# Transformer layer with mixture of experts: the shared expert in plain fp32, the second norm and the router's tail rearranged

## The chip, the cores and the metric

One core of a Trainium2 chip runs the kernel. The metric is the device time of the whole program in microseconds; three runs of the kernel before gave 993.31, 994.20 and 994.36 us, median 994.2 us.

## The reference

One pre-norm transformer layer over 2048 tokens of width 128, in fp32. Biases and weight scales are as drawn.

```python
x = x + attn(layernorm(x), qkv_w, qkv_b, out_w, out_b)       # 16 heads of 64, causal softmax
x = x + ffn(layernorm(x), gate_w, expert_*, shared_*)

def _ffn(x, gw, uw, dw):                                     # width 352
    return jax.nn.silu(x @ gw.T) * (x @ uw.T) @ dw.T
shared = _ffn(xf, shared_gate, shared_up, shared_down)
probs = softmax(xf @ gate_w.T)                               # 8 experts
topw, topi = top_k(probs, 2); topw = topw / (topw.sum(-1) + 1e-20)
out = shared + sum over the two chosen experts of topw * _ffn(xf, expert weights)
```

## The kernel before

The residual is held feature-major (128 features on the partitions, 2048 tokens along the free axis, four blocks of 512). Products that need fp32 accuracy are made of three matmuls in fp32r, whose operands are split into a high and a low part (`mm3`: high x high, high x low, low x high).

**Attention.** The loop over 16 heads (`for h in range(H)`) runs over 20 groups of two key tiles each (`GROUPS`). TensorE writes scores into `st`, which has two halves (`STRING`), so it can be two groups ahead; ScalarE makes the exponential twice, in fp32 and fp16; GpSimd subtracts one from the other (`p_low`); three groups later (`LAG`) TensorE multiplies by V (`p_times_v`). Beside that, `SLOTS[h][n]` lists by hand the background tasks of each place. Each task uses one of three banks of `bg` in turn, made on TensorE and drained on VectorE in the order of `TASKS`; a bank is used anew when the third task before has been drained (`bg_drained`). In the last head (`LAST_HEAD`), where there is no next head to prepare, all tasks stand behind both scores of their group and ahead of its mask.

**Last head.** For a block of 512 tokens: `att_t` (transposes the last pair's attention rows; waits for `normalise`), `att_y` (output projection, added to `res`), `turn` (transposes `res` to token-major; VectorE takes the statistics and copies it back into `res`), `inverse_deviation` (the second norm's factor by two Newton steps, on VectorE, for 8 tiles at once), `normal_rows`, `rows_t` (transposes the normalised rows back, split into high and low part), `logits`, `router_top`, `ranks` (positions of the tokens in their expert's list, by matmuls with a triangle and ones), `places`. `second_copy` makes a copy of the rows for the second chosen expert. Each row has two more words: its number and its weight (`ROW` = 130).

**Shared expert.** 12 steps (`STEPS`, four blocks by three chunks of 128 hidden features): gate and up by `mm3`, SiLU on ScalarE, `hidden` on VectorE, `hidden_hi` on ScalarE, `hidden_lo` on VectorE, `down` by `mm3` two steps later, `shared_copy`, and `base`: transposed and added to `res`. The rest of the tasks of blocks 2 and 3 are placed between the steps. GpSimd then scatters the rows with indirect DMAs (`scatter_rows(g)`, 16 for each half of the tokens) to lists in DRAM by expert. `early_table` and `late_table` make the table of the 39 tiles: the expert and the first row of each; the first `EARLY` = 9 of them are from the first half alone.

**Expert tiles.** For each of 39 tiles of 128 rows: SP gathers it (`XRING` = 8 buffers; gather i waits until the result of tile i-8 has been stored), TensorE transposes it, gate and up, SiLU, product, transposes, down; the result is scaled by the row's weight and scattered to `y_dram` by GpSimd (`scatter_y`). At the end SP loads the results in four parts, VectorE adds two rows for each token, and SP stores.

Of the kernel before, what the change touches and what calls it, by code (L numbers as in the profile page):

```python
# [12 lines left out]
F32, F32R = mybir.dt.float32, mybir.dt.float32r  # L13
# [23 lines left out]
HRING, SRING = 2, 2  # L37
# [4 lines left out]
XRING, YRING, AHEAD = 8, 12, 2  # L42
SKIP = 8192
ROW = P + 2
# [4 lines left out]
FILLS = 8  # L49

# [46 lines left out]
def background(h):  # L97
# [17 lines left out]
    if h + 1 < H:  # L115
# [19 lines left out]
TAIL = [("ranks", 0), ("att_t", PAIRS - 1, 3), ("att_y", PAIRS - 1, 3), ("turn", 2), ("turn", 3), ("rows_t", 2),  # L135
        ("rows_t", 3), ("base", 0), ("logits", 1), ("base", 1), ("ranks", 1), ("base", 2), ("base", 3)]
# [15 lines left out]
def layer_kernel(nc, x_t, qkv_w, qk_bias_in, v_bias, out_w, out_bias, gate_w_t, ffn_w, out_rows):  # L152
    ctx = ExitStack()
    with ctx:
# [57 lines left out]
        lg = sb("lg", [P, NT, EXPERTS], F32)  # L212
        lg_max = sb("lg_max", [P, NT, 1], F32)
        pr = sb("pr", [P, NT, EXPERTS], F32)
# [3 lines left out]
        top_atf = sb("top_atf", [P, NT, 2], F32)  # L218
        top_w = sb("top_w", [P, NT, 2], F32)
        wsum = sb("wsum", [P, NT, 1], F32)  # L220
        hot = sb("hot", [P, 2, NT, EXPERTS], F32)

        shared_hi = sb("shared_hi", [P, 3 * FC * P], F32R)
        shared_lo = sb("shared_lo", [P, 3 * FC * P], F32R)
# [8 lines left out]
        newton = sb("newton", [P, 3, 8], F32)  # L233
        shifted = sb("shifted", [P, 8], U32)
# [3 lines left out]
        chosen_sum = sb("chosen_sum", [P, 3, EXPERTS], F32)  # L238
        ones = sb("ones", [P, P], F32)
        tri = sb("tri", [P, P], F32)  # L240
# [12 lines left out]
        shared_raw = pflat[:, 2 * 2 * BLK:2 * 2 * BLK + 3 * FC * P]  # L253


        second = [v_words[0][:, 4 * ROW * b:4 * ROW * (b + 1)] for b in range(NB - 1)] + [high_words[:, 0:4 * ROW]]
        second = [x.rearrange("p (t c) -> p t c", c=ROW) for x in second]
# [3 lines left out]
        chosen = wo_flat[:, 0:P].rearrange("p (t e) -> p t e", e=EXPERTS)  # L261
        slot_at = wo_flat[:, P:2 * P].rearrange("p (t e) -> p t e", e=EXPERTS)
        hot_slot = wo_flat[:, 2 * P:4 * P].rearrange("p (r t e) -> p r t e", r=2, e=EXPERTS)
        reach = wo_flat[:, 4 * P:5 * P].rearrange("p (e j) -> p e j", e=EXPERTS)
        ends_by = wo_flat[:, 5 * P:5 * P + DUMP * EXPERTS].rearrange("p (i e) -> p i e", e=EXPERTS)
# [4 lines left out]
        place = wr_flat[0][:, 96:128].rearrange("p (r t) -> p r t", r=2)  # L270
        tiles_past = wr_flat[0][:, 192:192 + DUMP]
        row_sum = wr_flat[0][:, 240:240 + DUMP]
        row_base = wr_flat[0][:, 288:297]
        row_step = wr_flat[0][:, 304:312]
        taken = wr_flat[0][:, 312:320]
        gap = wr_flat[0][:, 320:329]
        count_now = wr_flat[0][:, 344:352]
# [3 lines left out]
        h_hi = [split_flat[:, k * BLK:(k + 1) * BLK] for k in range(HRING)]  # L281
        h_lo = [stage_parts[:, k * BLK:(k + 1) * BLK] for k in range(HRING)]
# [4 lines left out]
        shared_t = low_words[:, YRING * P:YRING * P + BLK]  # L287
        t_y_low = [high_words[:, 4 * ROW + k * P:4 * ROW + (k + 1) * P] for k in range(2)]
# [8 lines left out]
        t_x_hi = [shared_hi[:, k * P:(k + 1) * P] for k in range(2)]  # L297
        t_x_lo = [shared_hi[:, (2 + k) * P:(3 + k) * P] for k in range(2)]
# [37 lines left out]
        router_max, router, router_exp = sem("router_max"), sem("router"), sem("router_exp")  # L336
        shared_landed, shared_hi_ready, shared_lo_ready = sem("shared_landed"), sem("shared_hi_ready"), sem("shared_lo_ready")
# [3 lines left out]
        ln_stats, ln_rows, rows_ready = sem("ln_stats"), sem("ln_rows"), sem("rows_ready")  # L341
        turned_copied, hot_ready, places_ready = sem("turned_copied"), sem("hot_ready"), sem("places_ready")
        table_ready, shared_copied = sem("table_ready"), sem("shared_copied")
# [7 lines left out]
        y_landed, y_added, out_ready = [sem(f"y_landed{b}") for b in range(NB)], sem("y_added"), sem("out_ready")  # L351
        gu_ready, silu_done, h_ready = sem("gu_ready"), sem("silu_done"), sem("h_ready")
        h_hi_ready, h_lo_ready, down_done = sem("h_hi_ready"), sem("h_lo_ready"), sem("down_done")
# [21 lines left out]
        def v_quad(slot, q, lo, hi):  # L375
            return v_parts[slot][:, :, 4 * q:4 * q + 4, lo:hi]
        def stage_width(j):
            return F if j < 2 else FC * P
# [10 lines left out]
        def tiles_of(g):  # L389
            return slice(8 * g, 8 * g + 8)  # L390

# [4 lines left out]
        def _(sp):  # L396
# [13 lines left out]
            sp.dma_start(shared_raw, ffn_w[SHARED, :, :]).then_inc(shared_landed, 16)  # L410

            def spread_head(h):

# [1092 lines left out]
```

## Time and profile before

| | us |
|---|---|
| median of three runs | 994.2 |
| the profiled execution | 994.17 |
| its span | 992.4 |
| TensorE busy (share) | 924.8 (93%) |
| VectorE busy | 740.9 (75%) |
| GpSimd busy | 729.9 (74%) |
| ScalarE busy | 713.3 (72%) |

Fifteen heads take up to 761.7 us, the last head up to 817.6, the shared expert with the router's tail up to 884.5, the tiles up to 977.6, and the end is 14.8 us. A busy share is a mean over these; a wait row names the instruction that waited, and the one that released it. A matmul's duration in the rows contains its drain, which overlaps the next one: the distance between two starts is the pace. A fp32 matmul shows as two records.

### The profile page before, as it was taken

The page shows a single profiled execution, that of the slowest core. Times are in us where ns is not written, and L with a number is a line of the kernel's source. Part 1 is how long each engine was busy: PE and PEld are TensorE (multiplying, and loading weights), DVE is VectorE, ACT ScalarE, POOL GpSimd, SP SyncE. Part 2 cuts the span into 40 slices and gives each one's busy share as a digit, 9 for nine tenths or more (in the row PEclk, how much of TensorE's full clock was granted, in tenths as well). Part 3 has the DMA queues.
Part 4 walks back from the last instruction along what each step waited for, and adds up shares of the span by engine and source line. Part 5 has one row for each costly group of instructions (what it writes and reads, how often), then busy time and mean ns, then how long its engine had stood idle before and what let it go on. Part 6 is the DMA issues. An engine that isn't in the chain of part 4 may idle for free. (4 is left out here: it accounts for less than half of the span.)

```text
span 992.4 us, 25979 instructions
## 1 busy us (share of the span) xinstructions
PE 924.8 (93%) x10330; PEld 776.1 (78%) x10330; DVE 740.9 (75%) x1775; ACT 713.3 (72%) x891; POOL 729.9 (74%) x460
## 2 busy tenths in 40 slices
PE   7889999999999999999999999999999787779992
PEld 5458888888888888888888888888887575669992
DVE  4978797878878786978797868778784667756664
ACT  4048888888888888788888888898889752335661
POOL 1328888888898888888989888898889845064442
PEclk8879999999999999999999999999999978879996
DMA  3321434343544444535414040404032015111214
GB/s 104 85 64 23 94 77 118 78 109 78 118 88 99 98 112 104 124 84 122 105 39 111 31 110 25 117 25 102 6 83 99 39 69 192 31 44 52 58 56 135
DMA packets 70103, 82.03 MB, mean 83 GB/s; under 512 B 8784, under 2 KB 53970, under 8 KB 67936
## 3 DMA queue, kind: packets, MB, share of 16 engines
q1 hardware_dynamic: 67712, 76.14, 31.1%
q0 software_dynamic: 2272, 4.24, 1.2%
q8 instruction: 84, 1.38, 0.6%
q14 instruction: 35, 0.29, 0.1%
HBM read 21.81 MB, written 25.30 MB: 47 GB/s over the span
## 5 line engine op out<-in xcount | busy, mean ns | idle before, releaser
L583 POOL TENSOR_TENSOR p_lo<-prob,p_hi 128x1024 f16<-128x1024 f32 x320 | 617.5, 1947 | 136.9 <-ACT p_hi L685 135.7
L684 ACT ACTIVATE prob<-st,p_bias 128x1024 f32<-128x1024 f32 x320 | 329.7, 1030 | 124.4 <-PE st L1276 98.0
L685 ACT ACTIVATE p_hi<-st,p_bias 128x1024 f16<-128x1024 f32 x320 | 327.7, 1024 | 0.0
L979 DVE TENSOR_REDUCE row_max<-bg 128x1 f32<-128x512 f32 x384 | 255.4, 685 | 14.6 <-PE bg L1201 9.1
L1275 PE MATMUL st<-big 128*128 128x512 f32 (+3 forms) x640 | 242.8, 382 | 3.0 <-ACT p_hi L685 1.7
L1201 PE MATMUL bg<-big 128*128 128x512 f32 (+3 forms) x640 | 236.5, 400 | 4.5 <-DVE v_parts L969 2.1
L1307 PE MATMUL pv<-v_parts,p_hi 128*128 128x65 f16 x2176 | 235.9, 194 | 1.8 <-POOL p_lo L583 1.8
L1307 PEld LDWEIGHTS pv<-v_parts,p_hi 128*128 128x128 f16 x2176 | 200.5, 96 | 45.5 <-issue 32.6
L1309 PE MATMUL pv<-v_parts,p_hi 128*128 128x64 f16 x2176 | 234.6, 195 | 0.0
L1276 PE MATMUL st<-big 65*128 65x512 f32 (+3 forms) x640 | 233.2, 370 | 0.0
L1311 PE MATMUL pv<-v_parts,p_lo 128*128 128x65 f16 x2176 | 233.0, 192 | 0.0
L1311 PEld LDWEIGHTS pv<-v_parts,p_lo 128*128 128x128 f16 x2176 | 203.4, 99 | 0.0
L1309 PEld LDWEIGHTS pv<-v_parts,p_hi 128*128 128x128 f16 x2176 | 203.1, 97 | 0.2
L1201 PEld LDWEIGHTS bg<-big 128*128 128x128 f32 x640 | 124.0, 194 | 33.7 <-DVE row_max L979 7.7
L1275 PEld LDWEIGHTS st<-big 128*128 128x128 f32 x640 | 122.9, 192 | 19.0 <-ACT p_hi L685 2.8
L1276 PEld LDWEIGHTS st<-big 65*128 65x128 f32 x640 | 122.3, 191 | 17.8
L975 DVE CUSTOM_DVE_ANT_0 junk<-bg,mask_wide 128x128 bf16<-128x128 f32 (+3 forms) x256 | 121.9, 483 | 9.6 <-PE bg L1201 8.4
L959 DVE TENSOR_SCALAR big<-bg,qk_bias 128x512 fp32r<-128x512 f32 x64 | 48.0, 750 | 68.3 <-PE bg L1154 68.3
L618 POOL DMA_INDIRECT y_dram<-p_lo,v_parts x39 | 37.8, 970 | 50.2 <-DVE p_lo L1123 50.2
L961 DVE SCALAR_TENSOR_TENSOR big<-bg,qk_bias,big 128x512 fp32r<-128x512 f32 x64 | 48.1, 751 | 2.3
L611 POOL DMA_INDIRECT row_dram<-attn,place_u x16 | 16.3, 1017 | 35.6 <-DVE place_u L893 23.4
L1132 DVE TENSOR_TENSOR prob<-prob,st 128x352 f32<-128x352 f32 x39 | 20.3, 521 | 28.5 <-ACT prob L759 28.5
(224 smaller groups left out, 1227.9 us busy)
## 6 DMA issues: line engine op xcount, KB each, us to landing
big<-big SPq DMA_DIRECT2D x192, 128.0 KB, 2.3
row_dram<-fill SPq DMA_DIRECT2D x8, 1300.0 KB, 9.4
big<-part_dram SPq DMA_DIRECT2D x8, 1088.0 KB, 7.8
big<-big SPq DMA_DIRECT2D x16, 512.0 KB, 4.3
part_dram<-stage_parts SPq DMA_DIRECT2D x32, 176.0 KB, 3.2
part_dram<-stage_parts SPq DMA_DIRECT2D x16, 192.0 KB, 3.8
stage_raw<-ffn_w SPq DMA_DIRECT2D x16, 176.0 KB, 3.0
v_parts<-row_dram SPq DMA_DIRECT2D x39, 65.0 KB, 1.8
```

What stands on the lines that cost most here:

```text
L583: nc.gpsimd.tensor_tensor(o, a, b, ALU.subtract).then_inc(p_lo_ready, 1)
L684: nc.scalar.activation(o32, src, ACT.Exp, bias=p_bias[:], scale=D ** -0.5)
L685: nc.scalar.activation(o16, src, ACT.Exp, bias=p_bias[:], scale=D ** -0.5).then_inc(exp_done, 1)
L961: nc.vector.scalar_tensor_tensor(out=q_lo_shift[s][:, blk(b)], in0=bank, scalar=bias, in1=k_lohi[s][:, blk(b)].bitcast(F32), op0=ALU.add, ...
L975: nc.vector.tensor_tensor_reduce(masked[k % BGRING][:, 0:width], bank[:, 0:width], mask_wide[:, BLK - width:BLK], 1.0, -3.0e38, ALU.add, A ...
L979: nc.vector.tensor_reduce(row_max[:, t, c:c + 1], bank, AX_X, ALU.max).then_inc(bg_drained, 1)
L1201: mm = nc.tensor.matmul(bank[:, 0:width], q_hihi[s][:, tile(t)], k_lohi[s][:, c * BLK:c * BLK + width], start=True, stop=True)
L1275: nc.tensor.matmul(out, k_lohi[s][:, tile(kt)], q_hihi[s][:, q], start=True, stop=False)
L1276: mm = nc.tensor.matmul(out, k_hi_one[s][0:D + 1, tile(kt)], q_lo_shift[s][0:D + 1, q], start=False, stop=not diagonal)
L1307: nc.tensor.matmul(out, p_hi[:, n % PRING, cols], v[:, 0:D + 1], start=(kt == 0 and j == 0), stop=False, skip_group_check=True)
L1309: nc.tensor.matmul(out[:, 0:D], p_hi[:, n % PRING, cols], v[:, D + 1:VW], start=False, stop=False, skip_group_check=True)
L1311: mm = nc.tensor.matmul(out, p_lo[:, n % PRING, cols], v[:, 0:D + 1], start=False, stop=(kt == 4 * b + j), skip_group_check=True)
```

## The change

- The shared expert's gate, up and down products are made in fp32, one matmul for three: `shared_hi`, `shared_lo`, `h_hi`, `h_lo` and the operations that made them go; `shared_w` comes. The hidden ring `HRING` is 3.
- The result of the down product is added to `res` while that is feature-major (`base_sum`, VectorE); `base` then transposes the sum, and ScalarE copies it to `res` (`base_copy`). `turn` no longer writes `res`.
- The last pair's output projection is one fp32 matmul (`att_whole`).
- The second norm: `turn` itself makes the inverse deviation of blocks 0 and 1, each for four tiles with intermediate results in a PSUM bank, and the normalised rows from PSUM. Blocks 2 and 3 are done together in `turn` 3. `rows_t` makes only `xn`, no high and low parts; for blocks 2 and 3 ScalarE copies.
- The router takes the two largest logits themselves from PSUM; `router_exps` and the weights are computed once, after the tiles, and applied to the results at the end. Rows have 129 words. `ranks` works in bf16; `places` has fewer steps.
- The tasks have other places: `LAST_HEAD` starts one place earlier, with `ranks` 0 and `turn` 2 in it; the steps of the shared expert are written out by hand. The late table is made in tile 2 of the expert tiles.
- `XRING` is 12. The end works in eight chunks (`CHUNKS`), with 32 scaled additions. The last expert's weights are loaded without a wait for `att_y`. `second_copy` is ScalarE's, and the scatters go first over the first choices, then over the second.

```diff
-HRING, SRING = 2, 2
+HRING, SRING = 3, 2
-XRING, YRING, AHEAD = 8, 12, 2
+XRING, YRING, AHEAD = 12, 12, 2
-LAST_HEAD = {6: [("att_t", PAIRS - 1, 0)], 7: [("att_y", PAIRS - 1, 0)], 8: [("turn", 0)],
-             9: [("att_t", PAIRS - 1, 1)], 10: [("att_y", PAIRS - 1, 1)], 11: [("turn", 1)],
-             13: [("rows_t", 0)], 15: [("rows_t", 1)], 16: [("att_t", PAIRS - 1, 2), ("logits", 0)],
-             17: [("att_y", PAIRS - 1, 2)]}
+LAST_HEAD = {5: [("att_t", PAIRS - 1, 0)], 6: [("att_y", PAIRS - 1, 0)], 7: [("turn", 0)],
+             9: [("att_t", PAIRS - 1, 1), ("rows_t", 0)], 10: [("att_y", PAIRS - 1, 1)], 11: [("turn", 1)],
+             13: [("rows_t", 1)], 15: [("att_t", PAIRS - 1, 2)], 16: [("logits", 0)], 17: [("att_y", PAIRS - 1, 2)],
+             18: [("ranks", 0)], 19: [("turn", 2)]}
...
+            def inverse_deviation(t0, n, scratch):
+                t = slice(t0, t0 + n)
+                aside = [newton[:, 2 + k, 0:n] if scratch is None else scratch[:, 8 * k:8 * k + n] for k in range(3)]
+                variance, halved, copy = aside
+                own(nc.vector.tensor_scalar(variance, mean_var[:, t, 1], EPS, None, ALU.add))
...
+                y, square = newton[:, 0, 0:n], halved
+                for k, constant in enumerate(RSQRT_STEPS):
+                    other = y
+                    if scratch is not None:
+                        other = copy
+                        own(nc.vector.tensor_copy(copy, y))
+                    own(nc.vector.tensor_tensor(square, other, y, ALU.mult))
+                    own(nc.vector.tensor_tensor(square, square, var_half[:, 0:n], ALU.mult))
...
+                    if b < 2:
+                        att = ("att_y", PAIRS - 1, b)
+                        inverse_deviation(4 * b, 4, bg[:, NUMBER[att] % BGRING]).then_inc(bg_drained, 1)
+                        dve.wait_ge(bg_drained, drained(att))
+                        rows_of(attn, bank, b).then_inc(bg_drained, 1)
...
-                mm3(pv[:, :], shared_hi[:, d], shared_lo[:, d], h_hi[q % HRING], h_lo[q % HRING],
-                    c == 0, c == FC - 1).then_inc(down_done, 1)
+                nc.tensor.matmul(pv[:, :], shared_w[:, (2 * FC + c) * P:(2 * FC + c + 1) * P], h32[q % HRING], start=(c == 0),
+                                 stop=(c == FC - 1)).then_inc(down_done, 1)
...
-                mm3(st[:, q % 2, 0, :], shared_hi[:, g], shared_lo[:, g], xn_hi[:, blk(b)], xn_lo[:, blk(b)], True, True)
-                mm3(st[:, q % 2, 1, :], shared_hi[:, u], shared_lo[:, u], xn_hi[:, blk(b)], xn_lo[:, blk(b)], True, True
-                    ).then_inc(gu_ready, 1)
+                nc.tensor.matmul(st[:, q % 2, 0, :], shared_w[:, g], xn[:, blk(b)], start=True, stop=True)
+                nc.tensor.matmul(st[:, q % 2, 1, :], shared_w[:, u], xn[:, blk(b)], start=True, stop=True
+                                 ).then_inc(gu_ready, 1)
...
+            def base_sum(b):
+                dve.wait_ge(down_done, FC * (b + 1))
+                nc.vector.tensor_tensor(res[:, blk(b)], res[:, blk(b)], pv[:, :], ALU.add).then_inc(shared_summed, 1)
...
+            router_weights()
+            rows = res[:, :].rearrange("p (t d) -> p t d", d=P)
+            for c in range(CHUNKS):
+                dve.wait_ge(y_landed[c], 16)
+                for r in range(2):
+                    for t in range(NT)[chunk(c)]:
+                        last = nc.vector.scalar_tensor_tensor(out=rows[:, t], in0=y_rows[:, t, r, :], scalar=top_w[:, t, r:r + 1],
+                                                              in1=rows[:, t], op0=ALU.mult, op1=ALU.add)
```

The new order on TensorE in the shared expert, written out: gate/up 0, att_t 3, gate/up 1, att_y 3, gate/up 2, turn 3, down 0, gate/up 3, down 1, gate/up 4, down 2, gate/up 5, rows_t 2, rows_t 3, down 3, down 4, logits 1, down 5, gate/up 6, gate/up 7, ranks 1, down 6, base 0, gate/up 8, down 7, base 1, gate/up 9, down 8, gate/up 10, down 9, base 2, gate/up 11, down 10, down 11, base 3.

## Rows read from the trace of the kernel before

**Rows 1.** Windows: stretch, length, busy of PE, PEld, DVE, ACT, POOL, clock, DMA.
```profile
761.70:817.60 55.90, 44.52 (x605) 37.36 (x602) 32.34 (x98) 39.51 (x42) 40.58 (x22) 0.88 0.22 83
817.60:884.50 66.90, 46.34 (x209) 36.31 (x205) 46.29 (x174) 20.75 (x36) 27.92 (x28) 0.86 0.28 100
884.50:977.60 93.10, 87.90 (x623) 84.53 (x622) 57.32 (x155) 53.89 (x155) 41.66 (x44) 0.96 0.18 51
977.60:992.40 14.80, 0.00 (x0) 0.00 (x0) 5.53 (x8) 0.00 (x0) 0.94 (x1) 0.50 0.69 213
```

**Rows 2.** Waits, 758 to 822: who waited for whom, total us, times, longest.
```profile
ACT prob L684 <- PE st L1276: 12.4, 6, 8.5
...
PE bg L1228 <- DVE attn L824: 6.8, 1, 6.8
...
ACT prob L684 <- PE st L1288: 2.6, 3, 2.2
```

**Rows 3.** Timeline, last head: start, us, engine, line, operation.
```profile
789.34 4.20 POOL L583 TENSOR_TENSOR p_lo<-prob,p_hi 128x1024 f16<-128x1024 f32 x2 [0.29 <-ACT p_hi L685]
789.52 1.97 DVE L813 TENSOR_TENSOR newton<-newton 128x8 f32<-128x8 f32 x1
...
791.52 2.04 DVE L814 TENSOR_TENSOR newton<-newton,var_half 128x8 f32<-128x8 f32 x1
...
794.41 2.14 DVE L824 TENSOR_SCALAR attn<-res,mean_var,rstd 128x128 f32<-128x128 f32 x8
```

**Rows 4.** Timeline, VectorE, shared expert: statistics and inverse deviation.
```profile
832.29 0.89 DVE L998 BATCH_NORM_STATS2 stats<-bg 128x6 f32<-128x128 f32 x4
...
836.46 0.17 DVE L813 TENSOR_TENSOR newton<-newton 128x8 f32<-128x8 f32 x1
```

**Rows 5.** The page's costliest groups: busy, mean ns; idle before, releaser.
```profile
L684 ACT ACTIVATE prob<-st,p_bias 128x1024 f32<-128x1024 f32 x320 | 329.7, 1030 | 124.4 <-PE st L1276 98.0
```

**Rows 6.** Timeline, TensorE: fp32 first norm and V, fp32r in the shared expert.
```profile
4.04 6.22 PE L1159 MATMUL st<-res,ones_mean 128*128 128x512 f32 x8 [4.04 <-DMA res<-x_t]
...
698.04 1.05 PE L1191 MATMUL bg<-w_raw,xn 128*128 128x128 f32 x8
...
824.02 0.40 PE L1153 MATMUL st<-xn_lo,shared_hi 128*128 128x512 f32 x1
...
824.26 0.40 PE L1154 MATMUL st<-xn_hi,shared_lo 128*128 128x512 f32 x1
```

**Rows 7.** Windows, two pieces at the lower clock, columns as in rows 1.
```profile
818.00:822.00 4.00, 4.00 (x19) 3.53 (x17) 1.50 (x8) 0.60 (x1) 0.00 (x0) 0.57 1.00 418
...
863.00:872.50 9.50, 9.21 (x32) 8.18 (x33) 4.65 (x16) 1.10 (x2) 1.95 (x3) 0.50 0.15 39
```

**Rows 8.** Timeline, GpSimd: second half's first scatter, stores of tiles 0, 11, 12, 38.
```profile
869.95 0.97 POOL L611 DMA_INDIRECT row_dram<-attn,place_u  x1 [23.43 <-DVE place_u L893]
...
893.41 0.97 POOL L618 DMA_INDIRECT y_dram<-p_lo,v_parts  x1 [2.92 <-DVE p_lo L1123]
...
918.69 0.97 POOL L618 DMA_INDIRECT y_dram<-p_lo,v_parts  x1 [1.13 <-DVE p_lo L1123]
920.79 0.97 POOL L618 DMA_INDIRECT y_dram<-p_lo,v_parts  x1 [1.13 <-DVE p_lo L1123]
...
977.57 0.97 POOL L618 DMA_INDIRECT y_dram<-p_lo,v_parts  x1 [1.32 <-DVE p_lo L1123]
```

**Rows 9.** Timeline of the end: loads of the results, first and last additions.
```profile
979.83 2.03 SPq L503 DMA_DIRECT2D big<-y_dram  x4
983.81 0.69 DVE L1143 TENSOR_TENSOR res<-res,big 128x512 f32<-128x512 f32 x1 [7.01 <-DMA big<-y_dram]
...
989.01 0.69 DVE L1145 TENSOR_TENSOR res<-res,big 128x512 f32<-128x512 f32 x1
```

**Rows 10.** Groups by line, 817 to 884.2: busy, mean ns, idle before and releaser.
```profile
L1070 DVE TENSOR_TENSOR stage_parts<-prob,split 128x512 fp32r<-128x512 f32 x12 | 8.2, 684 | 1.7 <-ACT split L716 1.7
```

More of the change, by code:

```diff
@@ L134 @@
 PROLOGUE += [("v", 0, q) for q in range(4)] + max_tasks(0) + [("shift", 0)]
-TAIL = [("ranks", 0), ("att_t", PAIRS - 1, 3), ("att_y", PAIRS - 1, 3), ("turn", 2), ("turn", 3), ("rows_t", 2),
-        ("rows_t", 3), ("base", 0), ("logits", 1), ("base", 1), ("ranks", 1), ("base", 2), ("base", 3)]
+TAIL = [("att_t", PAIRS - 1, 3), ("att_y", PAIRS - 1, 3), ("turn", 3), ("rows_t", 2), ("rows_t", 3), ("logits", 1),
+        ("ranks", 1), ("base", 0), ("base", 1), ("base", 2), ("base", 3)]
 STAGED = [(e, j) for e in range(EXPERTS) for j in range(3)]
@@ L482, in _ @@
             sp.wait_ge(st_ready, H * NG)
-            for e in range(3, 7):
+            for e in range(3, EXPERTS):
                 expert_weights(e)
-            sp.wait_ge(bg_ready, drained(("att_y", PAIRS - 1, 3)))
-            expert_weights(7)
             for i in range(TILES):
@@ L624, in _ @@
             pool.wait_ge(filled, 16 * FILLS)
-            for g in range(2):
-                scatter_rows(g)
+            scatter_rows(0)
+            scatter_rows(1)
             for i in range(TILES):
@@ new lines, in places @@
+                own(nc.vector.tensor_tensor(
+                    hot_slot, hot[:, g], bank[:, 0:8 * EXPERTS].rearrange("p (o t e) -> p o t e", o=1, e=EXPERTS).broadcast_to(
+                        [P, 2, 8, EXPERTS]), ALU.mult))
+                with nc.allow_low_precision(reason="one whole number and zeros"):
+                    nc.vector.tensor_reduce(place_u[:, :, t], hot_slot, AX_X, ALU.add).then_inc(places_ready, 1)
+                nc.vector.tensor_copy(count[g], bank[:, 8 * EXPERTS:9 * EXPERTS]).then_inc(bg_drained, 1)
@@ new lines, in _ @@
+            background_task(("turn", 3))
+            hidden(2)
+            hidden(3)
+            early_tiles()
+            hidden(4)
+            base_sum(0)
+            table(0, EARLY)
+            hidden(5)
+            background_task(("logits", 1))
+            hidden(6)
+            base_sum(1)
+            background_task(("ranks", 1))
+            hidden(7)
+            early_taken()
+            hidden(8)
+            hidden(9)
+            late_tiles()
+            hidden(10)
+            base_sum(2)
@@ L1110, in tile_x_lo @@
+            hidden(11)
+            base_sum(3)
             def tile_x_lo(i):
@@ L1253, in background_task @@
                     b = task[1]
[L1254 removed]
+                    pe.wait_ge(shared_summed, b + 1)
                     for t in range(4):
[L1256 removed]
+                        mm = nc.tensor.transpose(bank[:, tile(t)], res[:, tile(4 * b + t)], ident[:])
                     mm.then_inc(bg_ready, 1)
@@ new lines, in _ @@
+            background_task(("att_t", PAIRS - 1, 3))
+            gate_up_shared(1)
+            background_task(("att_y", PAIRS - 1, 3))
+            gate_up_shared(2)
+            background_task(("turn", 3))
+            down(0)
+            gate_up_shared(3)
+            down(1)
+            gate_up_shared(4)
+            down(2)
+            gate_up_shared(5)
+            background_task(("rows_t", 2))
+            background_task(("rows_t", 3))
+            down(3)
+            down(4)
+            background_task(("logits", 1))
@@ L1393, in _ @@
+            down(5)
+            gate_up_shared(6)
+            gate_up_shared(7)
+            background_task(("ranks", 1))
+            down(6)
+            background_task(("base", 0))
+            gate_up_shared(8)
+            down(7)
+            background_task(("base", 1))
+            gate_up_shared(9)
+            down(8)
+            gate_up_shared(10)
+            down(9)
             background_task(("base", 2))
-            for q in range(STEPS - FLAG, STEPS):
-                down(q)
+            gate_up_shared(11)
@@ L1396, in _ @@
+            down(10)
+            down(11)
             background_task(("base", 3))
```

518 lines of the change are left out of this document (222 added, 296 removed).

## The prediction

> **What bounds the kernel now.** I read four views in this order. First the busy time by stretch [rows 1]: up to 761.7 us TensorE is busy nearly all the time, and the change touches nothing there that anything waits for (one split of the output weights in head 13, the two splits of the shared weights at the start, long before their use). From 761.7 us on no engine is full. So the reader should look at four stretches: the last head (55.9 us), the shared expert with the router (66.9 us), the 39 expert tiles (93.1 us), the end (14.8 us). What counts in each is who waits for whom.
>
> In the last head, ScalarE waits for scores for 12.4 us and 2.6 us more [rows 2], 15.0 us together, and TensorE for the normalised rows (L824) for 6.8 us in one piece. The timeline of that piece [rows 3] shows why: inside the inverse deviation two operations on 128x8 take 1.97 and 2.04 us, while GpSimd runs its subtraction of 4.20 us for two. The same operation without GpSimd's subtraction takes 0.17 us [rows 4]. Both read both inputs from SBUF.
>
> In the second stretch TensorE is busy 46.3 of 66.9 us, VectorE 46.3 [rows 1]; work goes to and fro between three engines (gate, SiLU, product, high part, low part, down), and TensorE's granted clock falls to 0.5, its 1.2 GHz level, after each longer idle piece: 4 us at 818 and 9.5 us at 863 [rows 7]. In the third TensorE sets the pace (87.9 of 93.1 us busy).
>
> **The change part by part.** *Last head.* The inverse deviation of blocks 0 and 1 moves into the task that turns the block, keeps its intermediate results in a PSUM bank, and the normalised rows are read from PSUM too. So no operation of it has two SBUF inputs. 13 operations at 0.17 us and 0.03 between, 0.2 each [rows 4], are 2.6 us; with four bn_stats (0.89) [rows 4], their aggregation with its waits (taken as 0.6) and four rows at 0.27 (2.14 for eight, [rows 3]) the task is 5.5 us of VectorE. It comes twice now, at places 7 and 11, and the next block's normalise and transpose queue behind it on VectorE. TensorE can be two groups ahead (the two halves of the score banks), some 4 us of ScalarE, whose two exponentials of a full group are about 1.0 us each [rows 5]. I laid the tasks against these 2.0 us a group (the four figures are estimates from this laying out, not rows): att_t of block 1 waits for turn 0 and leaves ScalarE 3.4 us idle; rows_t 1 after turn 1 1.8; logits and the unsplit att_y at 16 and 17 1.3; the ranks at 18, now ahead of the mask of a diagonal group, 1.4. Sum 7.9 against 15.0: a gain of 7.1 us. Bounds: 3 if the small operations in PSUM cost 0.35 rather than 0.2 (no row shows VectorE writing such a result to PSUM; the nearest is the 0.17), 11 if the lead of two groups covers nearly all.
> The Trainium skill says the same as [rows 3] in "SBUF — State Buffer", Who interferes with whom: a VectorE instruction with two SBUF inputs contends with a GpSimd instruction that reads SBUF, and the later one waits for all of it. It would take the two stalls away completely, as the sum has it.
>
> *Shared expert.* Removed on VectorE: 12 low parts at 0.684 [rows 10] = 8.2 us; on ScalarE 12 high parts; four copies of the down result go, the four additions stay (now before the transpose, on VectorE), and ScalarE copies the transposed blocks back. Two exp table loads leave the middle. A step's way from gate to down loses two hops of about 0.7 us each.
> Added on TensorE: each group of three fp32r matmuls becomes one fp32 matmul. Three fp32r of 512 columns are issued 0.235 apart, 0.70 a group [rows 6]. A fp32 matmul: four of 128 columns show as eight records in 1.05 us at the full clock [rows 6]; without the last one's drain 0.111 a record, 0.22 a matmul, 0.88 for 512 columns. The other bound is the first norm's four of 512 in 6.22 us, 1.55 each [rows 6]. I take 0.88, since the stage mostly runs at the full clock. Twelve steps of two and one, 36 matmuls, are 31.7 us for 25.4 before: 6.3 us more on TensorE.
> The Trainium skill ("FP8 and Floating Point Precision", TensorE Precision Notes) has true fp32 at four passes through the array. That speaks against this change, three passes being replaced by four: 0.94 a matmul, and 2 us more than my sum.
> The rest of TensorE's work here: eight groups of four transposes 4.0, one att_y 0.9, logits 1.7, one rank task in bf16 instead of two in fp32 about 1.0: 7.6, estimates from the 128-column records of [rows 6] and the counts in the code. The first rank task is moved into the last head, and with it the first 16 scatters start right when GpSimd has its last subtraction done.
> Lower clock: two pieces, at the start (4 us) and after the wait for turn 3, instead of 17 us in all; fp32 and transposes lose half of each, 3.5 us. Idle: VectorE does turn 3 in about 6.5 us (eight rows, 11 small operations) ahead of hidden 2, and TensorE's step 4 waits for that: 3.6; the third block's sum before down 9: 2.1; small ones and the last sum, copy and first tile's parts 1.8. Sum 31.7+7.6+3.5+7.5 = 50.3, against 66.9 from the start of step 0 to the first tile's gate: a gain of 16.6. Bounds 8 (a third piece at the lower clock, and every idle piece half as long again) and 21.
>
> *Expert tiles.* The tiles come steadily 2.10 us apart (918.69 to 920.79), but 38 of them took 84.2 [rows 8]: 4.4 us are lost where a gather waits until the eighth tile before it has been stored. The second scatter of 16 starts at 869.95 and runs for 20 us, so the first store comes late (893.41). With 12 buffers and the second scatter done about 3 us before that store is wanted, these 4.4 go. The late half of the table moves into tile 2 on VectorE, eight small operations, the three on 240 elements at 0.4 or more, say 2.3 us over a slack of 0.7 (both estimates): 1.6 back. Gain 2.8; bounds 1 and 4. Scaling by the weight leaves the tiles; it was inside an operation that stays.
>
> *End.* The weights are now applied at the end: 32 operations on 128x128 for eight on 128x512. At about 0.2 to 0.24 each (the rows of 128x128 in [rows 3] are 0.27) with a wait per pass it is 1.0 us a chunk, 8.0 in all, on data that arrive from about 982.6 (four loads were issued from 979.83, the first half megabyte was used at 983.81, the last at 989.01 [rows 9]). Last addition at 990.6 for 989.7, and the last store is smaller: 0.7 us lost. Bounds: 1 gained, 3 lost. The exp and the five operations behind it fit in while the stores land.
>
> Total 7.1+16.6+2.8-0.7 = 25.8. The profiled execution took 994.17 (span 992.4, 1.8 around it), the median is 994.2, so the working holds for both: 968.4.
>
> **The rivals.** *TensorE becomes the bound at the lower clock.* The new order keeps it waiting in small pieces, and more of the stage runs at 1.2 GHz, as 9.5 us did at 863 [rows 7]. Each microsecond of it costs half. Twenty more of them cost 10: 978. For it: every fp32 matmul is longer. Against: the idle pieces get rarer.
> *Last head not cured.* The 5.5 us task sits in front of normalise twice; if ScalarE's 15.0 us only move to other places, 7.1 are missing: 975.5. For it: no slack in VectorE's order there.
> *More is gained.* The lead of two groups covers the turns (11), and the shared expert reaches 47 (20): with the tiles and the end as above 961.
> *Slower.* The fp32 work never brings the clock up. 36 matmuls at 1.55 to 1.7 are 59 us, with the rest at half rate, 74 for the stage: 7 lost, which eats the last head's 7.1, and the total stands near 992. From about 8 us at the lower clock inside the tiles beyond the 4 of now it is slower than before: 996. Against: the eight records in 1.05 us were fp32 at the full clock, though surrounded by other work; for: the 6.22 us.
> *The splits were hidden anyway.* Partly so: VectorE and ScalarE were busy 46 and 21 of 67 us [rows 1]. That is why the chain, and not the removed work, is counted; it is inside the bound of 8.
>
> **How the numbers follow.** Forecast (963 to 974) 0.53; lower clock (974 to 984) 0.19; last head not cured 0.10; more gained (955 to 963) 0.13; slower 0.03; no difference 0.02. Within 0.2%, 2 us, a measurement of this kernel can't tell from no change. Faster 0.95, same 0.02, slower 0.03. The range leaves out the ends of both sides: 959 to 981.
>
> **What would show it.** Right: no VectorE operation on 128x8 over 0.5 us in the last head, ScalarE's waits for scores there near 8 us; from the first shared gate to the first tile's gate about 50 us, fp32 records in pairs 0.43 apart; no gather waiting for a store after the first; the last addition 13 us after the last tile's store. Wrong: turn tasks much longer than 5.5 us; granted clock 0.5 for over 10 us in the shared stage; GpSimd's second scatter still running when the first tile is to be stored.

## The result and the profile after

The changed kernel took 968.97 us (median of 4 runs, 968.54 to 970.06), the kernel before, run beside it, 993.75 (991.82 to 994.36). The ratio is 0.9756, with an interval of 0.9739 to 0.9772: 24.8 us faster. Its profiled execution took 968.54 us, with a span of 966.7. The forecast was 968.4.

The windows of the changed kernel, in the same four stretches as [rows 1] (last head, shared expert with the router, expert tiles, end; columns as there):

```profile
761.60:811.80 50.20, 42.85 (x614) 35.73 (x611) 23.27 (x109) 39.15 (x41) 40.62 (x23) 0.97 0.24 88
811.80:861.60 49.80, 41.02 (x141) 19.96 (x137) 26.61 (x105) 12.56 (x23) 30.23 (x31) 0.96 0.41 144
861.60:950.00 88.40, 84.94 (x623) 82.36 (x622) 56.03 (x162) 50.92 (x156) 37.84 (x39) 0.98 0.17 49
950.00:966.70 16.70, 0.00 (x0) 0.00 (x0) 10.31 (x37) 0.55 (x2) 0.97 (x1) 0.50 0.61 188
```

Against [rows 1] the last head is 5.7 us shorter, the shared expert 17.1, the tiles 4.7, and the end is 1.9 longer. VectorE is busy 26.6 us of the shared stage instead of 46.3, ScalarE 12.6 instead of 20.8.

The last head, waits from 758 to 816 us (who waited for whom, total, times, longest), which answer to [rows 2]:

```profile
ACT prob L687 <- PE st L1296: 6.2, 2, 5.5
...
ACT prob L687 <- PE st L1284: 3.3, 4, 1.8
PE bg L1213 <- DVE attn L1040: 3.1, 1, 3.1
```

The largest of these waits in the timeline (start, us, engine, line, operation):

```profile
775.55 0.89 DVE L1007 BATCH_NORM_STATS2 stats<-bg 128x6 f32<-128x128 f32 x4 [1.51 <-PE bg L1230]
...
779.50 1.37 DVE L836 TENSOR_SCALAR attn<-bg,mean_var,rstd 128x128 f32<-128x128 f32 x4
...
780.99 0.42 DVE L1040 TENSOR_TENSOR attn<-pv,rden 128x256 f32<-128x256 f32 x1
...
781.56 0.63 PE L1213 MATMUL bg<-ident,attn 128*128 128x128 f32 x4 [3.07 <-DVE attn L1040]
...
783.90 0.78 PE L1283 MATMUL st<-big 128*128 128x512 f32 x1
...
785.55 1.12 PE L1219 MATMUL bg<-xn,wo_all 128*128 128x512 f32 x2
...
786.81 1.11 ACT L687 ACTIVATE prob<-st,p_bias 128x1024 f32<-128x1024 f32 x1 [5.48 <-PE st L1296]
```

The turn of block 0 runs from 775.55 to 780.87, TensorE waits 3.07 us behind it, and then its score matmul takes 0.78 us where it took 0.40 before: the granted clock has fallen to its lower level (1.2 GHz). ScalarE gets its scores 5.48 us late.

The shared stage on TensorE, with its three longest waits:

```profile
814.07 1.02 PE L1375 MATMUL st<-xn,shared_w 128*128 128x512 f32 x2
814.93 1.02 PE L1376 MATMUL st<-xn,shared_w 128*128 128x512 f32 x2
...
825.64 1.13 PE L1375 MATMUL st<-xn,shared_w 128*128 128x512 f32 x2 [3.24 <-DVE prob L1070]
826.60 1.81 PE L1376 MATMUL st<-xn,shared_w 128*128 128x512 f32 x2
...
828.21 1.91 PE L1365 MATMUL pv<-prob,shared_w 128*128 128x512 f32 x2
...
852.22 1.10 PE L1365 MATMUL pv<-prob,shared_w 128*128 128x512 f32 x2 [2.46 <-DVE prob L1070]
...
858.88 0.63 PE L1264 MATMUL bg<-ident,res 128*128 128x128 f32 x4 [0.87 <-DVE res L1076]
```

A fp32 matmul of 512 columns is two records, and the next one starts 0.86 us later. After the wait at 825.64 the first takes 0.96 us, and the next one, at 826.60, takes 1.61: the granted clock over 825.6 to 832.0 is 0.73. From 811.8 to 825.6 it is 1.00. The wait at 852.22 is put down to `hidden` (L1070), but TensorE also needs the third block's sum there (VectorE, L1076), which started at 851.44, took 0.68 and so ended last.

GpSimd's second scatter and its stores, which answer to [rows 8]:

```profile
842.52 0.97 POOL L609 DMA_INDIRECT row_dram<-attn,place_u  x1 [10.49 <-DVE place_u L893]
...
869.91 0.97 POOL L616 DMA_INDIRECT y_dram<-p_lo,v_parts  x1 [7.28 <-DVE p_lo L1117]
...
950.01 0.97 POOL L616 DMA_INDIRECT y_dram<-p_lo,v_parts  x1 [0.86 <-DVE p_lo L1117]
```

The scatter starts 27.4 us earlier and ends before the first store; the 38 intervals between stores take 80.1 us instead of 84.2. The end, which answers to [rows 9]:

```profile
952.23 3.96 SPq L504 DMA_DIRECT2D big<-y_dram  x8
955.01 9.49 DVE L1142 SCALAR_TENSOR_TENSOR res<-big,top_w,res 128x128 f32<-128x128 f32 x32 [3.17 <-DMA big<-y_dram]
956.30 8.60 SPq L507 DMA_DIRECT2D out_rows<-res  x8
```

The 32 operations follow one another every 0.297 us (9.49 for 32).

### The profile page after: what moved, and what is told of

It is laid out like the page before. It is cut to its first block, busy times and chain, and to the rows that moved or that the text cites. A ratio compares the mean times of both kernels' runs of the same rounds, so it can differ in the third digit from the quotient of the medians.

```text
span 966.7 us, 25810 instructions
## 1 busy us (share of the span) xinstructions
PE 915.7 (95%) x10271; PEld 757.0 (78%) x10271; DVE 716.6 (74%) x1755; ACT 701.6 (73%) x877; POOL 725.2 (75%) x457
## 4 chain that ended last, share of the span: by engine, by line
PE 85%; DVE 8%; ACT 2%; DMA 2%; issue 2%; SPq 0%; POOL 0%; DVEq 0%; POOLq 0%; ACTq 0%
PE bg L1203 14%; PE st L1283 13%; PE st L1284 13%; PE pv L1315 7%; PE pv L1317 7%; PE pv L1319 6%; PE bg L1193 3%; PE bg L1154 3%; PE bg L1155 2%; PE bg L1156 2%; PE bg L1213 2%; DVE row_max L981 2%; PE st L1296 2%; PE bg L1452 1%; PE bg L1443 1%
## 5 line engine op out<-in xcount | busy, mean ns | idle before, releaser
L1284 PEld LDWEIGHTS st<-big 65*128 65x128 f32 x640 | 121.9, 191 | 17.6
L616 POOL DMA_INDIRECT y_dram<-p_lo,v_parts x39 | 37.8, 970 | 50.5 <-DVE p_lo L1117 50.5
L762 ACT ACTIVATE prob<-st 128x352 f32<-128x352 f32 x39 | 18.1, 465 | 30.1 <-PE st L1434 30.1
## 6 DMA issues: line engine op xcount, KB each, us to landing
row_dram<-fill SPq DMA_DIRECT2D x8, 1290.0 KB, 10.8
```

The lines of the kernel that those rows point to most:

```text
L1284: mm = nc.tensor.matmul(out, k_hi_one[s][0:D + 1, tile(kt)], q_lo_shift[s][0:D + 1, q], start=False, stop=not diagonal)
```

## The experiments

The experiments ran in three groups, on chips where the kernel before took 999.4, 1001.1 and 1000.5 us, about 7 more than above. The changed kernel ran again in the second group.

**The changed kernel again.**

> The changed kernel itself once more, unaltered, so that the runs beside it and the four before it can be set against it and not only against the kernel before. It has been timed at a ratio of 0.9756 (0.9739 to 0.9772) to the kernel before. Theory: 0.974 to 0.977 here too, and the four earlier runs then stand 2 to 17 us above it or beside it: scratch_sbuf 0.9922 (+16 us), splits_back 0.9861 (+10), fp32r_three 0.9841 (+8), fp32r_one 0.9728 (-3). Rival: the ratio depends on the chip, and where the kernel before takes 999 us the changed one is nearer 0.983; then fp32r_three is level with it, splits_back costs 3 us and scratch_sbuf 9, as those three were expected to.

976.04 us (975.12 to 976.05), ratio 0.9746 (0.9720 to 0.9772): the first reading holds. The ratio is the same on this second chip, the absolute time is not. Of the 7.6 us between the two profiled spans 1.9 lie ahead of the shared expert and 4.8 in it. Its granted clock differs too, 0.93 over the stage for 0.96, and not in a fixed way: here the clock stays at 1.00 behind TensorE's wait of 3.44 us at 827.75 and is 0.72 from 857 to 863, behind the one of 2.46 us; in the first profile it was the other way round. In the following, comparisons with the changed kernel are by this run; those across groups are by the ratios.

**The small operations back in SBUF.** For the turns in the last head:

```diff
-                        inverse_deviation(4 * b, 4, bg[:, NUMBER[att] % BGRING]).then_inc(bg_drained, 1)
+                        inverse_deviation(4 * b, 4, None).then_inc(bg_drained, 1)
```

> The changed kernel, but the inverse deviations of blocks 0 and 1 keep their intermediate results in SBUF (11 small operations instead of 13). Theory (a small VectorE operation whose inputs both lie in SBUF waits for GpSimd's running subtraction): at least two operations in each of the two turn tasks take 1 to 2 us instead of 0.17, as in rows 3 of the kernel before; the task grows by 3 to 6 us, the head ends 4 to 9 us later, total 973 to 978. Rival (the small operations in the kernel before were slow for another reason, or the gain in the head came from the new places of the tasks alone): every such operation stays at 0.17 and the total is that of the changed kernel, 969, or 0.3 less for two operations fewer.

990.48 us, ratio 0.9922 (0.9891 to 0.9953). VectorE and GpSimd in the first turn:

```profile
777.82 6.31 POOL L578 TENSOR_TENSOR p_lo<-prob,p_hi 128x1024 f16<-128x1024 f32 x3 [0.46 <-ACT p_hi L688]
```
```profile
777.82 0.17 DVE L813 CAST newton<-newton 128x4 f32<-128x4 uint32 x1
778.02 1.99 DVE L814 TENSOR_SCALAR newton<-newton 128x4 uint32<-128x4 f32 x1
780.04 2.04 DVE L816 TENSOR_SCALAR var_half<-newton 128x4 f32<-128x4 f32 x1
782.12 2.03 DVE L823 TENSOR_TENSOR newton<-newton 128x4 f32<-128x4 f32 x1
784.19 0.16 DVE L824 TENSOR_TENSOR newton<-newton,var_half 128x4 f32<-128x4 f32 x1
```

As soon as GpSimd's subtractions start (three in 6.31 us), each operation on four columns takes about the length of one of them, and when they are over 0.16 again. In the second turn four operations are held, for 1.1 to 2.0 us each. The last head ends at 824.8 instead of 813.8, and ScalarE's longest wait is 11.1 us; the turn was expected to grow by 3 to 6 us and the head by 4 to 9. So the PSUM bank for the intermediate results is what lets the turn stand in the last head at all; without it 11 of the 25 us are gone there, and about 2 more in the shared stage. The profiled spans are these 13 us apart; the ratios make it 17.6, and where the rest lies is not shown.

**The splits back in the chain.** High and low part of the hidden values are computed again, as before, and TensorE waits for them, but multiplies in fp32:

```diff
+                nc.scalar.copy(h_hi[q % HRING], h32[q % HRING]).then_inc(h_hi_ready, 1)
+                nc.vector.tensor_tensor(h_lo[q % HRING], h32[q % HRING], h_hi[q % HRING], ALU.subtract
-                pe.wait_ge(h_ready, q + 1)
+                pe.wait_ge(h_lo_ready, q + 1)
```

> The changed kernel, with the high part of the hidden rows on ScalarE and the low part on VectorE put back into the way from product to down (they are computed, waited for, and not used). 12 times 0.61 on ScalarE and 12 times 0.69 on VectorE, in series. Theory (TensorE has the shorter queue and each hop is on the way only where TensorE waits for it; VectorE has about 20 us of slack in the stage, but its order is written out): 4 to 9 us slower, 973 to 978, with TensorE's waits for VectorE longer. Rival (the splits were hidden): within 1.5 us of the changed kernel.

985.95 us, ratio 0.9861 (0.9831 to 0.9892). The stage from the first gate to the first tile's gate is 65.4 us instead of 54.6. TensorE's down matmuls wait:

```profile
L1372 PE MATMUL pv<-prob,shared_w 128*128 128x512 f32 x24 | 15.8, 753 | 10.8 <-DVE xn_lo L1077 8.9 <-issue 1.9
```

(busy, mean ns; idle before them, releaser.) In the changed kernel again the same matmuls wait 3.2 us, so 7.6 of these 10.8 are new. The stage is longer by 10.8 us as well, which is another sum: TensorE idles 17.3 us in it instead of 11.7, and the same work keeps it busy for 48.1 us instead of 42.9, at a granted clock of 0.85 instead of 0.93. So two hops in each of twelve steps cost about 11 us (11.5 by the ratios), half as waits and half as the lower clock, in a stage in which VectorE and ScalarE are busy for only about half and a third. That is more than half of the stage's gain. It may be more: the changed kernel again has an unexplained idle piece in this stage (last section), and this run has none; against the 49.8 us of the first profile the stage is 15.6 longer.

**One and three fp32r matmuls instead of one fp32 matmul**, with inputs that are only rounded, not split; gate and up read the rows of the first norm. In the second the same product is added three times. So the shared expert's values are not the reference's; only times are read.

```diff
+                for k in range(3):
+                    mm = nc.tensor.matmul(pv[:, :], shared_r[:, (2 * FC + c) * P:(2 * FC + c + 1) * P], h32[q % HRING],
+                                          start=(c == 0 and k == 0), stop=(c == FC - 1 and k == 2))
```

> As fp32r_three, with one fp32r matmul instead of three (the result is wrong in the same way). TensorE's work in the stage falls by 36 times 0.62, 22 us. Theory (TensorE is the bound with some 6 us of waits): the stage falls from 50 to 33 to 38 us, limited then by VectorE (about 31 us of work) and the chain through the second norm and the router; total 953 to 957. Rival (chain): less than 5 us faster, 964 or more.

> The changed kernel, but each fp32 matmul of the shared expert is three fp32r matmuls on the same operands (nothing is split, so the low parts are left out; gate and up take the first norm's rows; both leave the result wrong and the waits as they are). It measures three passes against fp32. Theory (TensorE's work sets most of this stage): 36 times 0.86 less 0.70, 5.6 us less work, of which pieces beside the turn 3 and the sum before down 9 are hidden: 3 to 5 us faster than the changed kernel, about 965. Rival (the chain through three engines sets the stage): within 1 us of it, 968 to 969.

One: 972.28 us, ratio 0.9728 (0.9701 to 0.9754). Three: 983.64, ratio 0.9841 (0.9814 to 0.9869). Three is about 9 us slower than the changed kernel, with less work for TensorE. Windows of the shared stage in the changed kernel (again), with one, and with three:

```profile
813.80:868.40 54.60, 42.93 (x139) 20.71 (x135) 26.47 (x105) 12.55 (x23) 31.10 (x32) 0.93 0.37 133
```
```profile
812.30:858.30 46.00, 26.11 (x99) 18.53 (x98) 26.67 (x105) 12.46 (x23) 28.12 (x29) 0.67 0.42 152
```
```profile
813.60:876.10 62.50, 41.51 (x172) 31.88 (x170) 26.56 (x105) 12.35 (x23) 31.04 (x32) 0.78 0.32 116
```

With one, TensorE has 16.8 us less work, the stage is 8.6 us shorter at a granted clock of 0.67, and only 2 us arrive at the end by the ratios, whose intervals overlap, since the first tile's store comes 14.0 us after its gate instead of 9.0. That is not TensorE's doing: ScalarE starts the first tile's SiLU late, with nothing in the profile that held it:

```profile
864.70 0.46 ACT L765 ACTIVATE prob<-st 128x352 f32<-128x352 f32 x1 [5.86 <-remote]
```

Half of what is taken from TensorE here is lost in the stage at once. The case that TensorE is the bound, 953 to 957, is out; that of the chain, 964 or more, holds. With three neither of the two expected cases came (3 to 5 us faster, or within 1 us). I took the clock as the cause there, and tested it with a fourth matmul, which brings TensorE's work back up (the edit is against the run with three).

```diff
-                for k in range(3):
+                for k in range(4):
```

> As fp32r_three, with a fourth fp32r matmul in each group, so that TensorE is as long at work as with one fp32 matmul (the inputs are only rounded, not split, so the result is less precise). fp32r_three came out at 0.9841, about 9 us above the changed kernel, though TensorE had less to do: its shared stage took 62.5 us against 54.6, at a granted clock of 0.78 against 0.93. Theory: the missing work is the cause; TensorE idles more often, the clock falls and everything behind it is late; with the fourth matmul the stage returns to 54 to 57 us and the ratio to 0.974 to 0.977. Rival: it is the form (three to four instructions where there was one, the weights rounded in another buffer), and a fourth costs its 0.235 us on top in each of 36 groups: stage 63 to 71 us, ratio 0.985 to 0.992.

991.09 us, ratio 0.9906 (0.9871 to 0.9940), stage 69.2 us at a clock of 0.81, with TensorE busy 50.5 us. That theory falls: filling TensorE did not bring the time back. The numbers lie in the range of the rival, that the fourth matmul costs its 0.235 us on top each time (36 times, 8.5 us; TensorE is busy 9.0 us more, the stage is 6.7 longer); it does not explain what three has lost. What three has more than the changed kernel is idle time that no other engine's work explains:

```profile
836.13 0.60 ACT L722 ACTIVATE prob<-st 128x512 f32<-128x512 f32 x1 [10.75 <-remote]
```
```profile
874.66 0.58 ACT L718 COPY res<-bg 128x512 f32<-128x512 f32 x1 [9.59 <-remote]
```

The scores of the first were ready at 829.4, the transposes of the second at 870.9. The run with four has two such waits (14.22 and 13.07 us idle). "Remote" stands where the profile has no releaser among the engines. More on it in the last section.

**The ring of gathered inputs alone**, in the kernel before and, the other way round, in the changed kernel:

```diff
-XRING, YRING, AHEAD = 8, 12, 2
+XRING, YRING, AHEAD = 12, 12, 2
```

> The kernel before, with the ring of gathered expert inputs at 12 instead of 8 slots, and nothing else changed. The prediction put 4.4 us of the gain down to stalls of the expert tiles that the longer ring takes away. Theory: 3 to 5 us below the kernel before, ratio 0.995 to 0.997. Rival: the stalls come from the late scatters and tables and not from the ring's length, and the ring alone does nothing: 0.999 to 1.001.

995.03 us, ratio 0.9952 (0.9931 to 0.9973): by the ratio 4.8 us below the kernel before. The first tile's SiLU, first and last store:

```profile
890.58 0.46 ACT L759 ACTIVATE prob<-st 128x352 f32<-128x352 f32 x1 [6.80 <-remote]
...
897.80 0.97 POOL L618 DMA_INDIRECT y_dram<-p_lo,v_parts  x1 [9.61 <-DVE p_lo L1123]
...
977.79 0.97 POOL L618 DMA_INDIRECT y_dram<-p_lo,v_parts  x1 [1.08 <-DVE p_lo L1123]
```

38 intervals take 80.0 us, against 84.2 in [rows 8]: the 4.2 us of stalls are gone. That they are the ring's alone is not shown, since here ScalarE was late with the first tile, and the first store starts 9.6 us after the last scatter has ended instead of 2.9. A late first store may let the gathers run ahead as well.

> The changed kernel with the ring of gathered expert inputs back at 8 slots instead of 12. In the changed kernel the tiles' stores come 2.10 us apart with no stall after the second; in the kernel before, with 8 slots, 38 intervals took 84.2 us, and with 12 slots alone 80.0. Theory: the stalls at every eighth or so tile come back, 2 to 4.5 us: ratio 0.977 to 0.979. Rival: the second scatter now ends 8 us before the first store instead of 3 before it, so the gathers run ahead anyway and the ring's length no longer matters: within 1 us, 0.974 to 0.976.

978.44 us (977.55 to 981.15), ratio 0.9796 (0.9755 to 0.9837). The interval holds both cases, but the stores decide: 877.86 to 958.97, 81.1 us against 80.0. With the second scatter done early (10.8 us ahead of the first store), 8 slots cost 1.1 us, not 4.2. So most of the stalls go without the longer ring once the scatter is done early; that the ring would have removed them by itself stays open.

**Two tasks of the last head moved.**

```diff
-LAST_HEAD = {5: [("att_t", PAIRS - 1, 0)], 6: [("att_y", PAIRS - 1, 0)], 7: [("turn", 0)],
-             9: [("att_t", PAIRS - 1, 1), ("rows_t", 0)], 10: [("att_y", PAIRS - 1, 1)], 11: [("turn", 1)],
-             13: [("rows_t", 1)], 15: [("att_t", PAIRS - 1, 2)], 16: [("logits", 0)], 17: [("att_y", PAIRS - 1, 2)],
+LAST_HEAD = {5: [("att_t", PAIRS - 1, 0)], 6: [("att_y", PAIRS - 1, 0), ("turn", 0)],
+             9: [("att_t", PAIRS - 1, 1)], 10: [("att_y", PAIRS - 1, 1)], 11: [("turn", 1)],
+             12: [("rows_t", 0)], 13: [("rows_t", 1)], 15: [("att_t", PAIRS - 1, 2)], 16: [("logits", 0)], 17: [("att_y", PAIRS - 1, 2)],
```

> The changed kernel, with two tasks of the last head moved: the turn of block 0 (5.3 us of VectorE) from place 7 to place 6, and the making of the rows of block 0 on TensorE and their four VectorE copies (1.37 each) from place 9 to place 12. Theory: the stall of 5.48 us at place 10 comes from the queue on VectorE of turn, rows and attention; with both moved it falls to 1 to 2 us, while the one at place 13 or 14 (1.78) may grow by up to 1.5: 2 to 4 us below after_again. Rival: the stall is that of the sum of VectorE's work over places 6 to 14, not of its order, and only moves on: within 1 us of after_again.

973.35 us (970.98 to 975.29), ratio 0.9715 (0.9686 to 0.9743), 2.7 below the changed kernel beside it. The last head's waits:

```profile
ACT prob L687 <- PE st L1284: 5.0, 5, 2.0
...
ACT prob L687 <- PE st L1296: 2.3, 3, 1.4
```

7.3 us in pieces of at most 2.0, against 11.1 with one of 5.5. The last head ends 3.5 us earlier, of which the profiled spans keep 1.3. The intervals of the two ratios overlap; the waits show that the stall was one of the order, since the sum falls and does not only move.

**The end on two engines.** ScalarE scales the second choice's rows, VectorE adds them:

```diff
+                    last = nc.scalar.activation(y_second[:, t, :], y_rows[:, t, 1, :], ACT.Copy, scale=top_w[:, t, 1:2])
-                for r in range(2):
+                nc.vector.tensor_tensor(rows[:, chunk(c)], rows[:, chunk(c)], y_second[:, chunk(c)], ALU.add
```

> The changed kernel, with the second choice's expert rows scaled by their weights on ScalarE into the retired buffer of the high parts, and added by one VectorE addition of 256 columns per chunk; VectorE keeps the multiply-and-add of the first choice. In the changed kernel the closing 32 multiply-and-adds took 9.49 us of VectorE (0.297 each), and ScalarE stood idle. Theory: VectorE's tail falls from 32 to 16 of them (4.7 us) and eight additions of about 0.3 to 0.6 us, 2.4 to 4.8 us; the tail is shorter by 1 to 2.5 us, since it cannot get ahead of the loads of expert rows: ratio 0.973 to 0.975, that is 1 to 2.5 us below after_again. Rival: the tail is set by the arrival of the expert rows and by the stores of the output (8.6 us of issuing), not by VectorE: within 0.5 us of after_again.

974.50 us (973.35 to 976.14), ratio 0.9739 (0.9713 to 0.9766). From the last tile's store to the end of the span it is 15.4 us (956.16 to 971.6) instead of 16.9 (957.45 to 974.3). In the time the two overlap; in the trace the end is 1.4 us shorter.

**VectorE's order in the shared stage, and all four edits.**

```diff
-            background_task(("turn", 3))
             hidden(2)
+            background_task(("turn", 3))
             hidden(3)
...
+            base_sum(2)
             late_tiles()
             hidden(10)
-            base_sum(2)
```

> The changed kernel with two changes of VectorE's order in the shared expert and nothing else. Hidden 2, whose SiLU is ready at 819.2 us, goes ahead of turn 3 (5.9 us of VectorE), and the third block's sum, for which TensorE waits at down 9 (2.46 us), goes ahead of the small operations that prepare the late tiles (2.1 us). Theory: the two waits of TensorE named in the prediction (3.24 us at gate 4, 2.46 at down 9) are these orders; the first falls to about 1.7 and moves to gate 5, the second goes, and with the pieces at the lower clock that follow them the stage is 3 to 6 us shorter: ratio 0.969 to 0.972. Rival: turn 3 itself is the bound, since rows 3 feed the last block's gate, and the logits and ranks behind it set the second scatter and the first tile; the waits move and the time falls by less than 1.5 us: 0.973 to 0.975.

> The changed kernel with four edits together: the two moved tasks of the last head (both_moves, 2.7 us below the changed kernel beside it), the end on two engines (end_act, 1.5), and on VectorE in the shared expert two changes of order: hidden 2 ahead of turn 3, and the third block's sum ahead of the preparation of the late tiles. Theory: the first two add up, since they lie in different stretches, and the two changes of order take away what vec_order is expected to take, 3 to 6 us: 7 to 10 us below the changed kernel, ratio 0.965 to 0.968. Rival: what is gained before the shared expert is waited for again inside it, at the gathers of the first tiles or at a wait on VectorE: 4 to 5 us below, ratio 0.970.

The order alone: 980.51 us (976.98 to 981.44), ratio 0.9796 (0.9754 to 0.9838), above both cases that were put for it. All four: 975.41 (973.39 to 977.26), ratio 0.9750 (0.9708 to 0.9793), no better than the two moves alone. The waits themselves behaved as expected: in the run with the order alone the one before a gate fell to 1.8 us, the one at down 9 went, and down 11 came 46.3 us after the last head's end instead of 49.7. Then, in the same run:

```profile
861.80 1.13 PE L1365 MATMUL pv<-prob,shared_w 128*128 128x512 f32 x2 [1.03 <-issue]
...
865.36 0.69 DVE L1076 TENSOR_TENSOR res<-res,pv 128x512 f32<-128x512 f32 x1 [3.61 <-remote]
866.19 1.09 PE L1264 MATMUL bg<-ident,res 128*128 128x128 f32 x4 [3.26 <-DVE res L1076]
...
868.81 0.97 POOL L609 DMA_INDIRECT row_dram<-v_parts,place_u  x1 [0.30 <-issue]
871.77 0.58 ACT L715 COPY res<-bg 128x512 f32<-128x512 f32 x1 [10.26 <-remote]
```

From down 11 to the first tile's gate it takes 11.6 us here, against 4.9 in the changed kernel. The sum starts 2.4 us after its product, the copy 4.5 us after its transposes, and nothing in the profile lies between. The 3.4 us gained were lost again, and 3.3 more.

## Why the prediction was right

The mechanism is right in the last head and the shared expert, and only in part in the tiles. That the total is right to a microsecond is luck in part, since errors cancel: 7.1+16.6+2.8-0.7 was forecast, 5.7+17.1+4.7-1.9 measured.

- *Last head, 7.1 forecast, 5.7 measured.* The turn came out as sized (5.5 forecast, 5.3 measured, small operations at 0.17 and 0.2 apart), with two errors that cancel: its terms add up to 5.2 and not 5.5, and the four rows took 1.37 instead of 1.07. ScalarE waits 9.5 us instead of 7.9. The mis-sized term is the stall at place 10, 5.48 for 3.4: I laid the tasks out at the full clock, and TensorE had stood idle for 3.07 us before and then worked at the lower one (0.62 over 781.5 to 786.0; what that costs is an estimate from this figure, 1.7 of the 2.1 us). At turn 1 it is 1.78 for 1.8.
- *Shared stage, 50.3 forecast, 49.8 measured.* The fp32 matmul goes by the steady records (0.86 for 0.88), not by the first norm's 1.55. The Trainium skill ("FP8 and Floating Point Precision", TensorE Precision Notes) gives fp32 four passes; 0.86 for 512 columns is 0.215 a pass by that. The trace agrees in size, as 0.86 is 3.7 times the 0.235 between fp32r matmuls, but cannot count passes. The sum of 0.94 was too high, since I had taken the pass at these 0.235. The waits were named and sized: 3.24 for 3.6 behind turn 3, 2.46 for 2.1 before down 9. Errors cancel here too: the lower clock was set at 3.5 us for two pieces, and only the one behind turn 3 came, about half of that; the ranks took 0.4 of the 1.0 us set for them; all idle time was 8.8 instead of 7.5.
- That the removed splits were on the path was argued, and is now shown by splits_back: the stage is 10.8 us longer with them. The rival that had them hidden is out, and so is the one of a lasting lower clock: 0.96 over the stage, 0.93 when run again.
- *Tiles, 2.8 forecast, 4.7 measured.* Of this 4.1 are the intervals between stores and 0.6 the way to the first one. The stalls were put at 4.4 and are gone; the late table costs 1.1 instead of 1.6 (the first three intervals are 3.33, 1.77 and 2.31 instead of 2.1 each). The cause is in part open: the early scatter is nearly enough in the changed kernel (xring8: 1.1), and whether the ring is enough in the kernel before is not shown, since in before_xring12 the first store was late too.
- *End, 0.7 forecast, 1.9 measured.* The step that failed is the price of the multiply-and-add on 128x128: taken at 0.2 to 0.24, where [rows 3] had 0.27 for an operation of that size with less input, and it is 0.297. 1.19 us a chunk instead of 1.0, over eight chunks 1.5 us.
- *Last head not cured* was the nearest rival; both_moves shows that the largest of the waits left was one of the order of the tasks.

## What to carry to other kernels

In a stage where work passes from engine to engine, count the hops and not the busy time: removing two hops of each step was worth about 11 us, though the matmuls that replace them take 0.86 us instead of 0.70. Small operations of VectorE beside large ones of GpSimd belong where GpSimd does not read: a PSUM bank for a few values per row was worth 11 us in the last head. An idle piece of TensorE can cost a second time at the lower clock, but need not: of the same two waits, 3.2 to 3.4 us and 2.5 us long, it followed the first in one execution and the second in the other. And two edits can remove the same stall: once the scatter is early, the longer ring is worth 1.1 us.

## What the runs showed of the hardware that was not expected

**Idle time that ends with a scatter.** On all chips but the first, though not in every run, ScalarE or VectorE stood still for 1 to 7 us with nothing in the profile that held them, while GpSimd ran through its 16 indirect DMAs or just behind them, and ScalarE mostly went on 3.3 to 3.7 us after the start of the last one. In the changed kernel run again:

```profile
836.32 1.20 ACT L652 COPY xn<-bg 128x512 f32<-128x512 f32 x2 [5.96 <-remote]
```
```profile
832.96 0.97 POOL L609 DMA_INDIRECT row_dram<-v_parts,place_u  x1 [0.30 <-issue]
```

836.32 is 3.36 after 832.96, and the first four transposes had been done since about 833. With the two moves it is 832.78 after 829.40 (3.38), with the end on two engines 834.99 after 831.66 (3.33), in before_xring12 890.58 after 887.23 (3.35), with one fp32r matmul 864.70 after 861.06 (3.64), with three fp32r matmuls 836.13 after 832.70 (3.43) and 874.66 after 870.94 (3.72), with VectorE's order changed 871.77 after 868.81 (2.96). It is not always so: in scratch_sbuf a copy went on 1.7 us after the last one, and in the first profile of the changed kernel the same copy started at 832.42, 1.37 after the last one, without being held. In splits_back no wait in this stretch is marked so, and in xring8 only one of VectorE's (1.43 us). Where a step falls relative to a scatter may thus decide over several microseconds. It is the likely reason for what vec_order, best and fp32r_three lost and for the late first tile of fp32r_one and before_xring12, and may be a part of the 7 us between the chips. That is argued from coincidence in time, not shown: no run takes the scatters away or moves them alone, and what holds the engine stays open.

**Operations with one SBUF input were held too.** In scratch_sbuf L814 and L816, with one tensor input each, took 1.99 and 2.04 us beside GpSimd's subtraction, as L823 with two did (2.03). In the changed kernel an operation from SBUF into PSUM (L822) took 0.17 us beside the same subtraction. I had argued from two inputs alone, in the prediction too. The Trainium skill ("SBUF — State Buffer", Who interferes with whom) has both: beside the rule on two inputs it says that a tensor_scalar from SBUF to SBUF can run in a mode that takes the port pair shared with GpSimd. The trace agrees with both.
